# Two products of 256 moved columns in place of one of 512, in the slot logits and the expert features

## The reference

```
x_n    = l2norm(x_ln) * scale            # x_ln = layernorm(layernorm(x)) * gamma + beta
logits = einsum('bnd,des->bnes', x_n, l2norm(mu, 0))      # 16 experts x 128 slots = 2048 columns
dispatch = softmax(logits, over n);  combine = softmax(logits, over all e*s)
slot_in  = einsum('bnd,bnes->besd', x_ln, dispatch)
h        = gelu(einsum('besd,edh->besh', slot_in, W1) + b1)   # 64 hidden features per expert
out      = einsum('bsd,bns->bnd', (h @ W2 + b2) over all e*s, combine)
x = x + out
```

## Time and profile before

| | |
|---|---|
| time, median of 3 runs | 569.59 us (567.27 to 569.8) |
| profiled execution, span from first to last instruction | 560.9 us |
| the median less that span (start, end, and the difference between executions) | 8.7 us |
| PE busy | 501.4 us, 89% of the span |
| weight loads (PEld, beside the products) | 406.3 us, 72% |
| DVE, ACT, POOL busy | 422.3, 290.3, 148.5 us |
| mean granted clock of PE | 0.970 |

### The profile page before, as it was taken

How to read it: one execution, slowest core, us unless ns; L and a number is a source line. 1 busy time by engine, 2 the same in 40 slices (tenths; PEclk the granted TensorE clock), 3 DMA queues, 4 the chain that set the end, 5 groups by cost and what they waited for, 6 DMA issues and landing times.

```text
span 560.9 us, 14312 instructions
## 1 busy us (share of the span) xinstructions
PE 501.4 (89%) x5544; PEld 406.3 (72%) x5544; DVE 422.3 (75%) x823; ACT 290.3 (52%) x537; POOL 148.5 (26%) x248
## 2 busy tenths in 40 slices
PE   0676999987797878889999999999999999999997
PEld 0444666654565555668888898898889889888986
DVE  5788998896799999856866686686668668666854
ACT  1363656664354646635455635745563574556344
POOL 4329211518363832311211212111121211112100
PEclk9868999999698989999999999999999999999999
DMA  6500000006000200000000000000000000000000
GB/s 188 197 6 6 8 6 7 8 1 160 6 6 5 62 0 1 4 1 1 11 11 2 11 9 9 0 9 9 0 9 9 9 0 9 9 0 9 11 11 11
DMA packets 15665, 11.65 MB, mean 21 GB/s; under 512 B 7040, under 2 KB 15120, under 8 KB 15376
## 3 DMA queue, kind: packets, MB, share of 16 engines
q1 hardware_dynamic: 15632, 11.18, 6.7%
HBM read 9.08 MB, written 2.10 MB: 20 GB/s over the span
## 4 chain that ended last, share of the span: by engine, by line
PE 75%; DVE 16%; ACT 3%; issue 2%; SPq 1%; DMA 1%; POOL 0%; DVEq 0%; ACTq 0%
PE bank L915 13%; PE bank L917 12%; PE bank L916 12%; PE bank L1140 10%; PE bank L1155 6%; PE bank L1127 5%; DVE qkr L664 4%; PE bank L965 4%; PE bank L980 4%; PE bank L994 3%; DVE rc L694 3%; PE bank L1014 2%; DVE mx L677 2%; PE bank L1161 2%; DVE pb L682 2%
## 5 line engine op out<-in xcount | busy, mean ns | idle before, releaser
L462 ACT ACTIVATE pb<-pb 128x512 f32<-128x512 f32 x64 | 39.4, 632 | 64.2 <-DVE pb L682 64.2
L545 ACT COPY mu_raw<-bank 128x512 f32<-128x512 f32 x34 | 19.7, 588 | 98.4 <-PE bank L1127 98.4
L1140 PE MATMUL bank<-w_raw,eb 128*128 128x130 f32 x512 | 60.2, 275 | 1.0 <-DVE w_raw L815 0.9
L1140 PEld LDWEIGHTS bank<-w_raw,eb 128*128 128x128 f32 x512 | 58.5, 190 | 1.5 <-DVE w_raw L815 1.4
L551 ACT ACTIVATE pb<-pb 128x768 f32<-128x768 f32 (+1 forms) x48 | 37.1, 774 | 40.1 <-DVE pb L844 40.1
L915 PE MATMUL bank<-mun_h,xlT_l 128*128 128x512 f32 x128 | 51.9, 405 | 0.2 <-DVE xlT_l L806 0.2
L844 DVE TENSOR_TENSOR pb<-bank,rh 128x384 f32<-128x384 f32 x96 | 49.3, 513 | 3.3
L980 PEld LDWEIGHTS bank<-ident,pb 128*128 128x128 f32 x256 | 31.3, 156 | 27.7 <-issue 25.0
L980 PE MATMUL bank<-ident,pb 128*128 128x128 f32 x256 | 45.9, 309 | 5.8 <-ACT vb L479 3.6
L917 PE MATMUL bank<-mun_h,xlT_h 128*128 128x512 f32 x128 | 50.6, 395 | 0.0
L916 PE MATMUL bank<-mun_l,xlT_h 128*128 128x512 f32 x128 | 50.5, 395 | 0.0
(11 more groups left out here) (156 smaller groups left out, 1261.2 us busy)
## 6 DMA issues: line engine op xcount, KB each, us to landing
mu_raw<-in_L_ffn_mu SPq DMA_DIRECT2D x1, 2048.0 KB, 12.8
out<-w_raw SPq DMA_DIRECT2D x16, 128.0 KB, 1.7
xa<-in_x SPq DMA_DIRECT2D x1, 1536.0 KB, 8.4
ctile<-in_ctx SPq DMA_DIRECT2D x16, 64.0 KB, 1.9
w_raw<-in_L_ffn_W SPq DMA_DIRECT2D x2, 512.0 KB, 5.3
w_raw<-in_L_ffn_W SPq DMA_DIRECT2D x1, 1024.0 KB, 9.1
xa<-in_x SPq DMA_DIRECT2D x1, 512.0 KB, 3.6
mu_raw<-in_L_ffn_b SPq DMA_DIRECT2D x1, 512.0 KB, 3.1
```

The costliest lines, as they stand in the source:

```text
L462: a.activation(pb[:, p, gr], pb[:, p, gr], ACT.Exp, scale=HD ** -0.5).then_inc(p_ready, 1)
L1140: m = mm(bank[HB[i % 3]][:, n * 2 * HC:(n + 1) * 2 * HC], eb[:, e, :], xw[:, e, :], start=True, stop=True)
```

## The change

Both bodies get an inner loop over the two halves of a bank. Each half takes 256 of the 512 columns, runs through both `k`, and writes its own half of the bank; the semaphore still goes up once, after the second half. The sums are the same. Per tile the 24 products of the slot logits become 48 and the 12 of the expert features 24, each with a weight load of its own.

```diff
+HALF = BANK // 2
@@ slot_logits
-                    for k in range(KD):
-                        m = mm3(bank[LB[c]][:], [h[:, k, :] for h in xlT],
-                                [h[:, k, c * BANK:(c + 1) * BANK] for h in mun], first=(k == 0), last=(k == KD - 1))
+                    for half in range(2):
+                        o = slice(half * HALF, (half + 1) * HALF)
+                        w = slice(c * BANK + half * HALF, c * BANK + (half + 1) * HALF)
+                        for k in range(KD):
+                            m = mm3(bank[LB[c]][:, o], [h[:, k, :] for h in xlT], [h[:, k, w] for h in mun],
+                                    first=(k == 0), last=(k == KD - 1))
                     m.then_inc(l_filled, 1)
@@ expand
-                    for k in range(KD):
-                        m = mm3(bank[2 + c][:], [h[:, k, :] for h in xlT],
-                                [h[:, k, c * BANK:(c + 1) * BANK] for h in w1], first=(k == 0), last=(k == KD - 1))
+                    for half in range(2):
+                        o = slice(half * HALF, (half + 1) * HALF)
+                        w = slice(c * BANK + half * HALF, c * BANK + (half + 1) * HALF)
+                        for k in range(KD):
+                            m = mm3(bank[2 + c][:, o], [h[:, k, :] for h in xlT], [h[:, k, w] for h in w1],
+                                    first=(k == 0), last=(k == KD - 1))
                     m.then_inc(xw_filled, 1)
```

## The result

Over 11 runs each, the kernel before has a median of 567.65 us (565.56 to 572.13) and the changed one 572.43 us (569.42 to 574.90). The ratio is 1.0058, with a 95% interval of 1.0030 to 1.0087: slower by 0.6%, or some 3.3 us (1.7 to 4.9). The forecast was +2.2 us (571.8), and the measurement is within its range and of the forecast sign.

The account below looks back on a forecast made before the run. PE was taken as the bound, at its upper clock from 265 us on. Slot logits +1.54, expert features of tiles 1 to 14 +0.67 and tile 15 +0.02 gave +2.2 us: 569.6 + 2.2 = 571.8 us, range 565.7 to 574.2.

Parts of the forecast that it names:

- Which of the two rows the new products resemble: 256-column pitch of the split products: taken as `project_qk`'s 118.6 ns, not `contract`'s 113.3, because of the stationary operand.
- the one 0.12 in the earlier trace: Last product of `contract`, with `xlT_l` loaded beneath it, takes 0.12 us against 0.11; read as `xlT` lengthening 256-column products.
- The size of a pair: Slot logits and expert features: two 256-column products cost 2 x 118.6 - 233.2 = +4.0 ns over the one replaced.
- "No wait is added": Semaphores: no wait added or taken away, each still rises after a whole bank, and nothing else becomes late.
- The prediction's own alarm: Middle tile's period: forecast wrong if it falls or grows by more than 0.25 us; 19.75 us expected instead of 19.6.
- The start modulo 64 as the reason: Conjecture: `xT` and `xlT` start 32 bytes off a multiple of 64, `gT` does not, hence the slower pitch.
- x fixed and y per 256 columns: Excess over column time: x + y = 12 and x + 2y = 20 ns, giving x = 4, y = 8.
- 1: New products run like `contract`: 113.3 ns, 226.7 per pair, -3.7 us, 565.9 us; chance 0.17.
- 2: Only a fixed cost is doubled, the transposes' 2.7 ns: +1.5 us, 571.1 us; chance 0.12.
- 3: Larger loop body leaves PE's instruction store, a stall at each jump back: 5.4 us beside the 2.2, 577 us; chance 0.05.
- 4: A pair costs just what the product did, the excess going with columns alone: 569.6 us; chance 0.06.
- Tile 0 and the end: Tile 0's expert features hide in a wait, nothing; in tile 15 only bank 2's six pairs count, +0.02 us.

Follow-up runs that it names:

- b_align: Kernel before with 32-byte pads ahead of `xT` and `gT`, so all stationary tiles start at 0 modulo 128; ratio to before 1.0004.
- only_logits: Kernel before with only the slot logits split into 256 columns, expert features left at 512; ratio to before 1.0020.
- only_expand: Kernel before with only the expert features split into 256 columns, slot logits left at 512; ratio to before 0.9985.
- b_gtoff: Kernel before with a 32-byte pad ahead of `gT`, moving its start from 64 to 96 modulo 128; ratio to before 1.0007.
- a_align: Changed kernel with 32-byte pads ahead of `xT` and `gT`, so all stationary tiles start at 0 modulo 128; ratio to before 1.0132.
- b_xl0: Kernel before, 512 columns kept, with pads putting `xlT` alone at 0 modulo 128; 565.81 us against 569.51, ratio 0.9945.
- a_xl64: Changed kernel with pads putting `xlT` alone at 64 modulo 128; ratio to before 0.9989.
- a_xl32: Changed kernel with pads putting `xlT` at 32 modulo 128, `gT` at 64; one run, tile period 19.760 us.

## Why the prediction was right, and where it was not

- *What bounds the kernel.* Right. The windows of 60 us are as full after as before, and every ns of pitch shows in the period.
- *Which of the two rows the new products resemble.* Right: 117.8 and 117.7 ns, near `project_qk`'s 118.6 and not `contract`'s 113.3. The argument from the one 0.12 in the earlier trace rows led to the right value. There is luck in it: `project_qk` stays at 118.5 with its operand at another start (b_align), and the same new products run at 116.7 or 116.5 where only one part is split (only_logits, only_expand), so that a pair costs within 0.2 ns of what the one product did.
- *The size of a pair.* +2.4 ns and not +4.0. The slot logits cost 0.060 us a tile and not 0.096, the expert features 0.029 and not 0.048: over the stage 1.3 us where the forecast had 2.2. The seven steps of the earlier trace rows are of a stream too short to settle; their mean over the 12 groups at the upper clock in the trace is 118.5, which would still have given +3.8.
- *"No wait is added", so all other steps stay as they are.* This is the step that failed. `contract` went from 113.3 to 117.8, +0.105 us a tile, some 1.6 us, more than the split products themselves. The sum had no term for it, and the earlier trace rows were read as the price of those products when they were one of two. The two errors, 0.9 us too much and 1.6 too little, partly cancel, and that the sum came so near (+2.2 against 2.85 in the stretch) is luck. The prediction's own alarm, a period that grows by more than 0.25 us, did not go off either: it grew by 0.194, of which 0.105 was something other than the pitch of the split products. That the loss is in the changed kernel and not in its one profiled execution alone is made likely by the runs: 1.3 us, the price of the split products alone, is below the interval of 1.7 to 4.9.
- *The start modulo 64 as the reason.* Marked a conjecture and wrong in its form: at a multiple of 64 the pitch is 113.3 or 117.8 (at 64) or 120.0 (at 0). That the start of the stationary tile matters at all is shown, by b_gtoff, b_align, a_align and b_xl0.
- *x fixed and y per 256 columns.* Fell: with the start at 0 two 256s take 240.0 and one 512 takes 226.7, x = 13.3 and y = 0; with it at 64 the two take 226.7 at best and the one 233.3, x = -6.6. That is just the fixed cost below nothing that the prediction had held against `contract`'s value. No such line exists.
- *The rivals.* 1: `contract`'s pitch is to be had, but not at this start, and it brought no gain (a_xl64, 19.613 us). 2: a fixed cost of 2.7 ns per product is nearer to the measured pair of +2.4 than the forecast's +4.0; yet the rows contradict it as a rule, by the values just named. 3: it did not come: 27 packets instead of 25, and no idle PE in the windows. 4: a pair at the price of the product is what each part shows when split alone, but not both together. Tile 0 and the end came out as read.

What stays open is the mechanism. Four of the steady values are whole multiples of 6.67 ns: 113.3 is 17 of them, 120.0 is 18, 226.7 is 34, 233.3 is 35; the columns alone would be 16 and 32. Two more fit only as averages, 117.8 as 53 of them in three steps and 116.7 as 35 in two, and the 118.2 to 118.4 of a_xl32 fit less plainly. 16 fp32 columns at 2.4 GHz take just that, 64 bytes in each partition. This fits two streams, weights and moving columns, that get in each other's way by pieces of 64 bytes, in a pattern of 128, and lock into a step. It is argued from the numbers, not shown.

## What to carry to other kernels

Where TensorE is the bound, the cost of a product in a row of products is not a constant of its form; the same 22 steps took 2.49 and 2.59 us in neighbouring tiles of one execution. So before a forecast takes a pitch from "the same form elsewhere", take it from a stream long enough to have settled, compare the start of the stationary tile against the moving one as well, and give the untouched streams of products an uncertainty of some 4% too. For an edit of 0.5%, compare the stretch of the trace that it touches, at one granted clock, product by product, and not the spans: here the spans differed by 9.9 us, of which 7 were the clock of an untouched stage.

## What the runs showed of the hardware

- Products in float32r with a 128 x 128 load each, at a granted clock of 1.00 (2.4 GHz), once settled: 256 columns 113.3 to 120.0 ns apart, 512 columns 226.7 to 233.3. A row of nine of 256 columns mostly does not settle: 118.5 on average with the start at 96 and at 0. The start of the stationary tile modulo 128, against moving tiles at 0, sorts them: at 0, 120.0 and 226.7 (after a run-in of five to ten products); at 64, 113.3 or 117.8, and 233.3; at 96, 116.5 to 117.8, and 233.2; at 32, 118.2 to 118.4.
- At 64 two rhythms exist, and one transpose more a tile ahead of the stream brought the fast one back and made the tile 0.07 us shorter; a smaller product in its place did not.
- At the lower clock, 1.2 GHz (granted 0.50 from 30 to 39 us in the kernel before), the inner products of the first `project_qk` come 213 to 214 ns apart for 256 columns, which is the columns alone; the excess was seen at the upper clock only.
